# Loads of turned attention weights to 32 target partitions each, and one store of 1 MB a round in place of two of 512 KB

## The reference

```
q, k, v = split_heads(x @ Wq.T), split_heads(x @ Wk.T), split_heads(x @ Wv.T)
a = einsum('bhnd,bhmd->bhnm', q, k) * 512 ** -0.5 + 2 * adj
a = where(any(a != 0, axis=-1), a, -inf)
p = softmax(a, axis=-1);  p = where(isnan(p), 0, p)
o = einsum('bhnm,bhmd->bhnd', p, v)
x = layernorm(x + merge_heads(o) @ Wo.T)
```

## Time and profile before

| what | value |
|---|---|
| time, median of 3 runs | 2162.87 us (2161.1 to 2163.74) |
| time of the profiled execution | 2158.4 us |
| its span in the trace | 2156.6 us |
| PE busy | 1841.4 us (85%) |
| DVE, ACT, POOL busy | 74%, 65%, 42% |
| DMA engines busy, mean of 16 | 51.6% (the queue of SP) |
| moved by DMA | 382.5 MB, 177 GB/s |
| granted PE clock, mean | 0.924 |

### The profile page before, as it was taken

How to read it: one execution, slowest core, us unless ns; L and a number is a source line. 1 busy time by engine, 2 the same in 40 slices (tenths; PEclk the granted TensorE clock), 3 DMA queues, 4 the chain that set the end, 5 groups by cost and what they waited for, 6 DMA issues and landing times. The chain is left out here.

```text
span 2156.6 us, 45319 instructions
## 1 busy us (share of the span) xinstructions
PE 1841.4 (85%) x14370; PEld 1479.6 (69%) x14370; DVE 1596.7 (74%) x5815; ACT 1398.7 (65%) x5134; POOL 905.7 (42%) x1516
## 2 busy tenths in 40 slices
PE   8888898889888888888888888898888988988885
PEld 6676676767676766766776766676666766766664
DVE  7777777777777777777777777777777777776774
ACT  6666666666666666666666666666666766666663
POOL 2244444444444444444444344444444444444432
PEclk9899999999999999999999999999998999999997
DMA  5455555555555555555555555545555555555443
GB/s 195 150 172 187 177 181 189 176 176 176 189 180 175 190 174 176 181 194 179 173 184 186 175 180 183 184 171 182 184 181 172 178 187 178 172 183 178 169 157 121
DMA packets 263183, 382.52 MB, mean 177 GB/s; under 512 B 12960, under 2 KB 143008, under 8 KB 262816
## 3 DMA queue, kind: packets, MB, share of 16 engines
q1 hardware_dynamic: 262368, 378.59, 51.6%
q10 hardware_dynamic: 576, 1.05, 0.1%
HBM read 212.86 MB, written 166.72 MB: 176 GB/s over the span
## 5 line engine op out<-in xcount | busy, mean ns | idle before, releaser
L700 ACT ACTIVATE e_sb<-neg_a,neg_max 128x128 f32<-128x128 f32 x2048 | 792.8, 391 | 157.5 <-DVE neg_max L852 157.5
L852 DVE CUSTOM_DVE_ANT_0 neg_a<-ps_s,adj_sb 128x128 f32<-128x128 f32 x2048 | 442.4, 286 | 237.7 <-PE ps_s L537 237.7
L470 PE MATMUL ps_w<-xt_hi,w_lo 128*128 128x512 f32 x1020 | 465.7, 457 | 0.0
L471 PE MATMUL ps_w<-xt_lo,w_hi 128*128 128x512 f32 x1020 | 443.2, 434 | 0.0
L557 PE MATMUL ps_o<-e_t,v_sb 128*32 128x128 f32 x4080 | 178.7, 329 | 299.2 <-DMA e_t<-blocks 299.2
L700 ACT ACTIVATION_READ_ACCUMULATOR e_sb<-neg_a,neg_max 128x1 f32 x2048 | 389.2, 190 | 0.0
L350 POOL TENSOR_TENSOR o_lo<-o_sb,o_hi 128x512 fp32r<-128x512 f32 x126 | 162.7, 1291 | 472.5 <-ACT o_sb L637 472.5
L557 PEld LDWEIGHTS ps_o<-e_t,v_sb 128*32 128x32 f32 x4080 | 137.5, 130 | 319.7 <-issue 318.1
L908 DVE STREAM_TRANSPOSE e_b<-e_sb 128x1024 f32<-128x1024 f32 x254 | 316.4, 1246 | 27.3 <-DVE e_sb L898 0.9
L366 POOL TENSOR_TENSOR x_sb<-y_sb,x_sb 128x512 f32<-128x512 f32 x122 | 155.0, 1270 | 415.9 <-ACT y_sb L637 415.9
L898 DVE SCALAR_TENSOR_TENSOR e_sb<-e_sb,r_inv 128x1024 f32<-128x1024 f32 x256 | 315.9, 1234 | 8.0 <-DVE r_inv L892 0.5
(11 more groups left out here) (104 smaller groups left out, 2861.6 us busy)
## 6 DMA issues: line engine op xcount, KB each, us to landing
blocks<-e_b SPq DMA_DIRECT2D x254, 512.0 KB, 7.9
e_t<-blocks SPq DMA_DIRECT2D x508, 256.0 KB
x_sb<-x SPq DMA_DIRECT2D x124, 256.0 KB, 6.6
out<-x_sb SPq DMA_DIRECT2D x124, 256.0 KB, 6.7
xt_raw<-xt SPq DMA_DIRECT2D x120, 256.0 KB, 6.4
adj_sb<-adj SPq DMA_DIRECT2D x32, 256.0 KB, 6.4
v_sb<-wk ACTq DMA_DIRECT2D x4, 256.0 KB, 6.3
neg_a<-xt SPq DMA_DIRECT2D x4, 256.0 KB, 5.9
```

What stands on the lines that cost most here:

```text
L470: pe.matmul(out, lhs_lo(c), rhs_hi(c), start=(c == 0), stop=False)
L471: pe.matmul(out, lhs_hi(c), rhs_lo(c), start=False, stop=False)
L700: last = act.activation(e_sb[:, i, h, :], neg_a[:, i, h, :], ACT.Exp, scale=-1.0, bias=neg_max[:, i, h:h + 1], accum_out=sums[:, i, h:h + 1])
L852: last = dve.tensor_tensor_reduce(out=neg_a[:, i, h, :], in0=ps_s[h][:, i * NODES:(i + 1) * NODES], in1=adj_sb[:, g % PAIR, i, :], scale=- ...
```

## The change

Loads: before, transfer a takes the scratch rows 32a to 32a + 31 and writes them to all 128 partitions of e_t, in the column range a; the DRAM side has the four blocks b outermost. Now transfer b writes the 32 partitions 32b to 32b + 31 of e_t, in all four column ranges, and both sides have the 32 rows outermost. The order of the four is 0, 2, 1, 3. Every contiguous run is 2 KB in both. Save: e_b and the scratch tensor have the two halves inside a block (b m r j), so the whole of e_b is saved in one transfer of 1 MB with runs of 8 KB, after both halves are turned. One semaphore `saved` takes the place of two; turning the first half now waits for the whole save of the phase before. Compute instructions stay, and stay in place.

```diff
-        blocks = e_b[:, :].rearrange("p (m b r j) -> p m r b j", m=2, b=BLOCKS, r=2 * TH)
-        blocks_half = e_b[:, :].rearrange("p (m b c) -> p m b c", m=2, b=BLOCKS)
+        blocks = e_b[:, :].rearrange("p (b m r j) -> p m r b j", m=2, b=BLOCKS, r=2 * TH)
...
-            def save_blocks(f, half):
-                sp.wait_ge(transposed, 2 * f + half + 1)
-                sp.dma_start(blocks_d[f % 2, :, :, half], blocks_half[:, half]
-                             ).then_inc(saved[half], 16)
+            def save_blocks(f):
+                sp.wait_ge(transposed, 2 * f + 2)
+                sp.dma_start(blocks_d[f % 2], e_b[:, :].rearrange("p (b c) -> p b c", b=BLOCKS)).then_inc(saved, 16)
 
             def move_blocks(f):
 
-                for half in range(2):
-                    sp.wait_ge(saved[half], 16 * (f + 1))
+                sp.wait_ge(saved, 16 * (f + 1))
                 if f:
                     sp.wait_ge(values_done, f)
                 else:
                     sp.wait_ge(xt_lo_done, CH)
-                width = GG * TH * NODES // BLOCKS
-                for a in range(BLOCKS):
-                    rows = slice(BLOCK * a, BLOCK * (a + 1))
-                    sp.dma_start(e_t[:, width * a:width * (a + 1)], blocks_d[f % 2, rows].rearrange("j b m c -> b j (m c)")
+                for b in (0, 2, 1, 3):
+                    rows = slice(BLOCK * b, BLOCK * (b + 1))
+                    sp.dma_start(e_t[rows, :].rearrange("p (a c) -> p a c", a=BLOCKS),
+                                 blocks_d[f % 2, :, b].rearrange("(a j) c -> j a c", a=BLOCKS)
                                  ).then_inc(moved, 16)
...
                 if f:
-                    save_blocks(f - 1, 1)
+                    save_blocks(f - 1)
...
-                if f < LAST:
-                    save_blocks(f, 0)
...
             def turn_blocks(f, half):
                 if f:
-                    dve.wait_ge(saved[half], 16 * f)
+                    dve.wait_ge(saved, 16 * f)
...
-    blocks = nc.dram_tensor("blocks", [2, P, BLOCKS, 2, 2 * TH * BLOCK], F32, kind="Internal").ap()
+    blocks = nc.dram_tensor("blocks", [2, P, BLOCKS, 2 * 2 * TH * BLOCK], F32, kind="Internal").ap()
```

More of the change, by code:

```diff
@@ L199, in build @@
         transposed = sem("transposed")
-        saved = [sem(f"saved{half}") for half in range(2)]
+        saved = sem("saved")
         moved = sem("moved")
```

## The result

| | before | changed |
|---|---|---|
| time, median (4 runs each) | 2163.3 us (2161.1 to 2167.52) | 1743.86 us (1742.78 to 1744.12) |
| ratio, 95% interval | | 0.8058 [0.8044, 0.8072] |
| span of the profiled execution | 2156.6 us | 1742.3 us |
| mean granted PE clock | 0.924 | 0.995 |

A forecast was written before the change was run, and what follows sets the result against it. The prediction took four loaded DMA engines as the bound. With them relieved, start to 107.6, 118 rounds of 13.3 us, two short rounds (21.1), a 42.2 us tail and 1.8 gave 1742 us, own range 1728 to 1765.

The forecast's parts named there:

- The bound: DMA queue: e_t loads run on four of sixteen engines, which need 16.7 us a round against the mean 16.4.
- Step 1: Loads by 32 target rows use sixteen engines; each engine then carries 9.4 us a round, below PE's 13.3.
- Step 2: One 1 MB save in place of two of 512 KB lands in 5.2 us (bounds 3.5 and 10.5).
- Step 3: DVE's first transposition waits for the whole previous save, with 4 us of cover; cost taken as nothing, at most 1.5 us.
- Step 4: Chain from transposition to values: loads 4.6 us, 10 us with the save, 13.4 us available, so 3.4 us spare.
- L: Time from a phase's second transposition ending to its loads' last landing; put at 10 us, upper 18.
- 3w = L - 13.4: Values on PE: if L exceeds 13.4 us, each round waits w; L = 18 gives w = 1.5 us.
- The sum: Whole program: start to round 7 at 107.6, 118 rounds of 13.3, two short rounds, tail 42.2, plus 1.8: 1742 us.
- A: Rival: the save-and-load chain stays too long, with waits up to 1.5 us a round; 1765 to 1919 us, chance 0.14.
- B: Rival: PE can't keep its clock without rests, so rounds take 14.3 us; 1860 us, chance 0.04.
- C: Rival: the loads' new shape reaches no more engines; 2158 to 2285 us, chance 0.05.
- D: Rival: 32 target rows take in too little, slower below 102 GB/s; 2330 us at 90 GB/s, chance 0.07.

The follow-up runs named there:

- e1: The changed kernel with the loads of before, so only the single 1 MB save is new: 2105.54 us, ratio 0.9757 to the kernel before.
- e5: e3 with one unused scratch row after each 32 rows: 2257.64 us, ratio 1.045 to the kernel before.
- e6: e5 with the unused row after each 16 rows instead and eight saves of 16 partitions: 1974.64 us, ratio 0.915 to the kernel before.
- e2: The kernel before with the new loads, keeping its two 512 KB saves and scratch layout: 1737.26 us, ratio 0.8045.
- e7: The changed kernel with the e_t loads issued right after the save, ahead of store, x, x turned and adj: 1744.79 us.
- e8: e2 with the e_t loads issued right after the second save, ahead of the store and the other loads: 1742.18 us.
- e3: The changed kernel with scratch laid out so each load writes all 128 partitions, and four saves of 32 source partitions: 1762.73 us, ratio 0.8166.

## Why the prediction was right

**The bound.** The four loaded engines were the bound: the pair with and without an unused row shows it, 1762.73 against 2257.64 us, and the shares 0.26, 0.51 and 1.01. How full they were is an estimate from each trace: 133.2 MB of loads at the rate behind their issue (99 to 101 GB/s, or 191), shared by four (or eight) engines, and what is left of the queue's busy time shared by sixteen. A loaded engine is then busy for 98% of the span in the kernel before and in e1, for 100% in the padded one (e5), but for 88% with eight engines (e6), where the chain is what binds.

**Step 1, sixteen engines for 32 rows.** Right. The size of what is left on them was a little off: the DMA share is 0.76 of a 13.3 us round, 10.1 us per engine, where the sum had 9.4. Behind the issue 229 GB/s pass, against the 146 for the load alone at which it would have counted; these include other traffic, so the loads' own rate isn't shown. That it didn't count is shown by the share of 0.76.

**Step 2, the save.** 4.4 us to landing (median; mean 4.8), 5.2 expected. That its effect on the time is nothing was wrong in both directions, which the halves show: with the old loads it brings 54 us (e1), with the new ones it costs some us (6 to 7 by e2, 2.6 between e7 and e8). The prediction saw only the second, as a longer chain with spare time.

**Step 3, DVE's wait.** Right: no row shows DVE waiting for a save in the changed kernel.

**Step 4, the chain.** The loads were mis-sized: from first issue to last landing 7.9 us (median; mean 8.0), not 4.6, so L was 12.8 (mean), not 10, and the spare 0.6 us, not 3.4. L passed 13.4 us in 19 rounds, and PE waited in 16 places, 12.6 us in all. Two terms had been left out: the three transfers ahead in the queue (0.9 us: 7.0 from first issue to last landing in e7) and the narrower target (up to 1.5 us: 6.4 in e3, which has other saves too). They make 2.4 of the 3.3 us; where the rest is stays open. The rule 3w = L - 13.4 holds with L as the traces have it (mean) to 0.1 us: it gives 2.3 (before, L = 20.4), 2.1 (e1, 19.6), 2.9 (e5, 22.0) and 1.3 (e6, 17.2), where PE waited 2.4, 2.1, 3.0 and 1.4 us a round. It says what a long chain costs, not what made it long.

**The sum.** Its marks against the changed kernel's timeline:

```profile
108.03 1.17 PE L532 MATMUL ps_s<-k_sb,q_sb 32*128 32x128 f32 x32
...
1678.33 1.17 PE L532 MATMUL ps_s<-k_sb,q_sb 32*128 32x128 f32 x32
...
1689.10 1.17 PE L532 MATMUL ps_s<-k_sb,q_sb 32*128 32x128 f32 x32 [0.17 <-issue]
...
1701.93 1.17 PE L532 MATMUL ps_s<-k_sb,q_sb 32*128 32x128 f32 x32 [1.61 <-issue]
```

Round 7 was to start at 107.6 and starts at 108.0; round 125 at 1677.0 and starts at 1678.3. Round 127 starts at 1701.9 for 1698.1: round 126 took 12.8 us for 10.6. DVE was busy for 12.4 of them, so it most likely binds there; the sum had let it bind at the start, where PE also has three products, and forgotten it at the end. The tail is 40.4 us for 42.2. So 3.8 us too few and 1.8 too many cancel in part. There is luck in the middle too: the sum took 13.3 us a round for the 13.26 of the row, which adds 4.7 us over 118 rounds, and the waits that step 4 had put at nothing cost 5.1 us between 100 and 1640 us. The forecast is thus nearer to the measured time than its terms are.

**The rivals.** A appeared weakly (12.6 us in all) in the changed kernel, and fully with eight engines. B fell: the clock is 1.00 over 1540 us of nearly unbroken work. C is what the padded kernel shows, 2258 us. D fell: the time is lower, with 229 GB/s behind the issue.

## What to carry to other kernels

Where DMA seems half busy and something still waits for it, look at the share right behind the issue of the transfer that is late: here 0.26 and 0.51 flat were four and eight of sixteen engines, and the outermost count of both sides is the first thing to read. While such a queue was the bound, one large save with larger runs paid (2.4%); once it wasn't, the length of the chain from the producer to the consumer counted, and two smaller saves, the first of them early, were a little faster than one large one. Before a transfer is moved ahead of others, look at who needs those others at the very end of the program.

## What the runs showed of the hardware that I had not expected

- One unused row of 2 KB after each 32 in DRAM turned a load over sixteen DMA engines into one over four, and the kernel from 1762.73 to 2257.64 us. The split went by the shape as it was built, not by the bytes.
- Loads into 32 partitions in the order 0, 1, 2, 3 instead of 0, 2, 1, 3 cost 14 us in this kernel (first issue to last landing 8.7 for 7.9 us); into all 128 partitions it was 6.4 us (e3, whose saves differ too).
- One save with 8 KB runs in place of two with 1 KB gave 2.4% back where the queue was bound by its engines (2105.54 for 2159.99 us), with no change in the loads' shape.
